# Recommendation tower with gathers, table looks and pairwise dot products: ten looked tables in eight straight-line groups of 256 samples, grams of one group placed between the looks of the next

## The reference, cut to what matters

```
e = stack([tbl_k[ids[:, k]] for k in range(26)], axis=1)        # 2048 x 26 x 128, fp32
combined = concat([dense[:, None, :], e], axis=1)               # 27 features of 128
inter = einsum('bnd,bmd->bnm', combined, combined)              # 27 x 27 a sample
z = concat([dense, inter[:, upper triangle]], axis=1)           # 351 pairs
h = concat([z, dense], axis=1)                                  # 607
h = relu(h @ W_top1 + b_top1)                                   # 512
h = relu(h @ W_top2 + b_top2)                                   # 256
y = h @ W_top3                                                  # 1
```

## Time and profile before

| what | value |
|---|---|
| median of 3 runs | 411.67 us (411.32 to 412.78) |
| the profiled execution | 414.85 us |
| its span, first to last instruction | 413.0 us |
| instructions in the profile | 14244 |
| mean granted TensorE clock | 0.971 |
| DMA traffic | 44.99 MB, mean 109 GB/s |
| packets under 512 B | 6198 of 20763 |

### The profile page before, as it was taken

One profiled execution on the slowest core, in us unless ns is written; L12 is line 12 of the kernel. 1 busy time (PEld: TensorE's weight loads), 2 busy tenths in 40 slices (PEclk: granted clock), 3 DMA queues, 4 the chain that ended last, 5 costly groups with the idle time before them and its releaser, 6 DMA issues.

```text
span 413.0 us, 14244 instructions
## 1 busy us (share of the span) xinstructions
PE 329.0 (80%) x6240; PEld 303.9 (74%) x6240; DVE 231.0 (56%) x234; ACT 142.9 (35%) x305; POOL 275.3 (67%) x295
## 2 busy tenths in 40 slices
PE   0300487999999999999989897989898895977676
PEld 0300486989898989897979796979888895966675
DVE  2244288686758676866666656576476656332211
ACT  1222216326333633363336231553236332442211
POOL 5777704777777777777777777777777777776000
PEclk9999998999999999999999998999999998998889
DMA  6444662254443434352424333342525142324020
GB/s 182 156 160 164 214 197 75 68 154 111 116 108 109 117 104 116 98 144 77 133 82 122 99 105 112 94 125 63 156 65 152 51 118 53 99 71 109 15 64 1
DMA packets 20763, 44.99 MB, mean 109 GB/s; under 512 B 6198, under 2 KB 11942, under 8 KB 20179
## 3 DMA queue, kind: packets, MB, share of 16 engines
q1 hardware_dynamic: 11524, 25.76, 20.3%
q0 software_dynamic: 9216, 18.89, 17.2%
HBM read 37.27 MB, written 7.36 MB: 108 GB/s over the span
## 4 chain that ended last, share of the span: by engine, by line
POOL 39%; PE 27%; issue 14%; DMA 7%; SPq 5%; ACT 4%; DVE 3%; POOLq 0%; ACTq 0%
POOL rows L294 39%; PE look_ps L333 11%; DMA grams<-in_table 6%; SPq L255 4%; PE gram_ps L354 4%; PE layer_ps L368 4%; PE layer_ps L379 3%; PE turn_ps L319 3%; ACT turned L576 2%; PE layer_ps L365 2%; DVE match L465 2%; DVE grams L451 1%; PE layer_ps L386 1%; DMA rows<-in_table,index 1%; ACT hidden L548 0%
## 5 line engine op out<-in xcount | busy, mean ns | idle before, releaser
L294 POOL DMA_INDIRECT rows<-in_table,index x288 | 274.5, 953 | 104.9 <-issue 86.5
L333 PE MATMUL look_ps<-match,table_high 125*128 125x256 f32 x512 | 137.9, 305 | 50.2 <-ACT looked_sb L564 27.7
L465 DVE TENSOR_TENSOR match<-look_ids,row_number_ps 125x2048 fp32r<-125x2048 int32 x64 | 145.8, 2280 | 6.5 <-DMA look_ids<-in_look_ids_rows 4.3
L333 PEld LDWEIGHTS look_ps<-match,table_high 125*128 125x128 f32 x512 | 103.2, 202 | 54.0 <-issue 52.4
L333 PE MATMUL look_ps<-match,table_low 125*128 125x256 f32 x512 | 132.2, 293 | 0.0
L333 PEld LDWEIGHTS look_ps<-match,table_low 125*128 125x128 f32 x512 | 103.8, 203 | 0.0
L451 DVE COPY grams<-gram_ps 27x432 f32<-27x432 f32 x64 | 38.2, 597 | 51.3 <-PE gram_ps L354 50.8
L319 PE MATMUL turn_ps<-identity,rows 128*128 128x128 f32 x288 | 47.2, 287 | 21.4 <-DMA rows<-in_table,index 21.3
L354 PE MATMUL gram_ps<-turned 128*27 128x27 f32 x4096 | 54.0, 194 | 5.1 <-issue 1.9
L354 PEld LDWEIGHTS gram_ps<-turned 128*27 128x27 f32 x4096 | 44.8, 105 | 15.4 <-issue 8.7
L368 PE MATMUL layer_ps<-pairs,w_pairs_sb 117*128 117x128 f32 x384 | 55.4, 282 | 0.0
(11 more groups left out here) (21 smaller groups left out, 101.8 us busy)
## 6 DMA issues: line engine op xcount, KB each, us to landing
look_ids<-in_look_ids_rows SPq DMA_DIRECT2D x16, 512.0 KB, 4.2
scratch<-grams SPq DMA_DIRECT2D x16, 364.5 KB
rows<-in_table,index POOLq DMA_INDIRECT x288
grams<-in_table SPq DMA_DIRECT2D x6, 500.0 KB
pairs<-scratch SPq DMA_DIRECT2D x48, 58.5 KB
scratch<-grams SPq DMA_DIRECT2D x16, 84.5 KB
dense_sb<-in_dense_t SPq DMA_DIRECT2D x1, 1024.0 KB, 5.0
turned<-in_table SPq DMA_DIRECT2D x2, 500.0 KB
```

The lines of the kernel that those rows point to most:

```text
L294: pool.indirect_dma_start(out=rows[u][:, group * GROUP_OF + n, :], out_offset=None, in_=tables[k], in_offset=bass.IndirectOffsetOnAxis(ap= ...
L333: last = nc.tensor.matmul(look_ps[:, 0:2 * P], part[0:look_rows, r, c, :], match[r % 2][0:look_rows, c, :], start=(c == 0 and part is tabl ...
L465: nc.vector.tensor_tensor(match[r % 2][0:look_rows], look_ids[0:look_rows, r].unsqueeze(1).broadcast_to(shape), row_number_ps[0:look_rows] ...
```

## The change

The order is new throughout, and so are the shapes:

- Ten tables are looked and 16 gathered. The features are reordered so that dense comes first, then the looked, then the gathered ones (`ORDER`), and the rows of `W_top1` with them.
- The unit of work is a group of 256 samples. There are eight, written out straight-line, with no loop in the program. `turned` exists twice, so looks are copied directly into it, two at a time from one of two PSUM banks.
- Transposed units and gram steps share three PSUM banks (`mid_ps`) in the order that `turn_number` and `gram_number` give. ScalarE makes all copies and activations; VectorE only matches and splits.
- A gram step still has 64 samples, now 16 from each quarter of the group, with 32 weight columns where 27 are features. So the four quadrants hold different samples, and `grams` is 128 partitions wide and exists once.
- The repack writes all 128 partitions (27 and 13 columns of 64 samples, 4 bytes each) and reads with 12 DMAs (3 chunks x 4 quadrants), each of 117 pieces of 64 samples. `scratch` and `pairs` exist once.
- Layers 1 to 3 run over 256 columns. The results are stored group by group.
- The raw tables are loaded in two parts, 112 and 13 partitions. The memory set aside for the descriptors of GpSimd's DMAs is 4096 bytes a partition.

```diff
-LOOKED = [8, 9, 10, 11, 15, 16, 17, 18]
+LOOKED = [8, 9, 10, 11, 15, 16, 17, 18, 19, 23]
+N = 256
+STEPS = 4
...
             def repack(g):
+                sp.wait_ge(mid_out, gram_number(g, STEPS - 1) + 1)
+                after(sp, pairs_in, PAIRS_DMAS * g)
+                flat = scratch.rearrange("s i j x -> (s i) j x")
+                sp.dma_start(flat[:, 0:FEATURES], grams[:]).then_inc(scratch_in, 16)
+                sp.dma_start(flat[:, FEATURES:WIDTH], grams[:, 0:SHIFTS]).then_inc(scratch_in, 16)
+                sp.wait_ge(scratch_in, SCRATCH_DMAS * (g + 1))
+                after(sp, layer1_done, 2 * g)
+                for c in range(CHUNKS):
+                    for s in range(QUADS):
+                        first = s * ROW * WIDTH + c * CHUNK_I * (WIDTH + 1) + 1
+                        skewed = bass.AP(scratch.tensor, first * IN_QUAD,
+                                         [[(WIDTH + 1) * IN_QUAD, CHUNK_I], [IN_QUAD, SHIFTS], [1, IN_QUAD]])
+                        sp.dma_start(pairs[0:CHUNK_ROWS, c, s * IN_QUAD:(s + 1) * IN_QUAD], skewed).then_inc(pairs_in, 16)
...
+            for j in range(groups * TILES):
+                for u in range(UNITS):
+                    after(pool, turn_done, UNITS * (j - 2) + u + 1)
...
+            def look(g, r):
+                pair = g * LOOK_PAIRS + r // 2
+                if g == 0:
+                    pe.wait_ge(tables_split, r + 1)
+                after(pe, looked, pair - 1)
+                pe.wait_ge(match_ready, g * LOOKS + r + 1)
...
+            def gram(g, k):
+                number = gram_number(g, k)
+                if k == 0:
+                    pe.wait_ge(mid_out, turn_number(g, TURNS - 1) + 1)
+                    pe.wait_ge(looked, LOOK_PAIRS * (g + 1))
+                    pe.wait_ge(dense_put, g + 1)
+                after(pe, mid_out, number - 2)
+                for i in range(IN_STEP):
+                    for s in range(QUADS):
+                        n = (s * IN_QUAD + k * IN_STEP + i) * FEATURES
+                        last = nc.tensor.matmul(
+                            mid_ps[number % 3][s * ROW:(s + 1) * ROW, i * FEATURES:(i + 1) * FEATURES],
+                            turned[g % 2][:, n:n + ROW], turned[g % 2][:, n:n + FEATURES], start=True, stop=True)
...
+            def layer1(g, o):
+                if o == 0:
+                    pe.wait_ge(pairs_in, PAIRS_DMAS * (g + 1))
...
+            for g in range(1, groups):
+                look(g, 0)
+                gram(g - 1, 0)
+                turn(g, 0)
+                look(g, 1)
+                gram(g - 1, 1)
+                turn(g, 1)
+                gram(g - 1, 2)
+                look(g, 2)
+                turn(g, 2)
+                gram(g - 1, 3)
+                look(g, 3)
+                turn(g, 3)
+                look(g, 4)
+                turn(g, 4)
+                look(g, 5)
+                turn(g, 5)
+                look(g, 6)
...
+                layer1(g - 1, 0)
+                layer1(g - 1, 1)
+                look(g, 7)
+                turn(g, 6)
+                layer1(g - 1, 2)
+                layer1(g - 1, 3)
+                look(g, 8)
+                turn(g, 7)
+                layer2(g - 1)
+                look(g, 9)
+                layer3(g - 1)
+            for k in range(STEPS):
+                gram(groups - 1, k)
+            for o in range(L1):
+                layer1(groups - 1, o)
+            layer2(groups - 1)
+            layer3(groups - 1)
```

More of the change, by code:

```diff
@@ L52, with build @@
 L2 = H2 // P
[L55 to L81, removed]
+def build(nc, dense_t, index_t, look_rows_t, tables, w1_dense, w1_pairs, b1, w2, b2, w3, y):
     fp32, fp32r, int32 = mybir.dt.float32, mybir.dt.float32r, mybir.dt.int32
@@ L85, in build @@
     batch = dense_t.shape[1]
[L86 to L92, removed]
+    groups = batch // N
+    table_rows = tables[LOOKED[0]].shape[0] // PARTS
+    assert batch % N == 0 and all(tables[k].shape[0] == table_rows * PARTS for k in LOOKED)
+    assert SPREAD < table_rows <= P and LOOKS % 2 == 0 and len(GATHERED) % UNIT_OF == 0 and FEATURES <= ROW
+    assert TURNS > STEPS and groups >= 2
     ctx = ExitStack()
@@ L388, in layer3 @@
                 last.then_inc(layer3_done, 1)
-            def tile(m, u, grams=True, layers=True, looks=True, last=False):
-                gm = m - 1 + u
-                for group in range(GROUPS):
-                    turn(m, u, group)
-                    if looks:
-                        for look_of in looks_after(m, u, group):
-                            look(*look_of)
-                    if grams and group < STEPS:
-                        gram(gm, 1 - u, group)
-                    if layers and group == AT_LAYER[0]:
-                        layer1(m - 1, u)
-                    if layers and group == AT_LAYER[1] and not last:
-                        layer2(m - 1, u)
-                    if layers and group == AT_LAYER[2] and not last:
-                        layer3(m - 1, u)
@@ L407, in _ @@
-            pe.wait_ge(identity_made, 1)
-            for r in range(EARLY):
-                look(0, r)
-            tile(0, 0, grams=False, layers=False)
-            tile(0, 1, layers=False)
-            pe.wait_ge(weights_summed, 1)
-            pe.wait_ge(dense_in, 16)
-            last_m = tiles // 2 - 1
-            with pe.Fori(1, last_m) as m:
-                tile(m, 0)
-                tile(m, 1)
-            tile(last_m, 0)
-            tile(last_m, 1, looks=False, last=True)
-            layer2(last_m - 1, 1)
@@ L623 @@
+            for k in range(STEPS):
+                take_gram(groups - 1, k)
+            for half in range(2):
+                relu1(groups - 1, half)
+            relu2(groups - 1)
+            copy_y(groups - 1)
 def kernel(**inputs):
```

600 lines of the change are left out of this document (266 added, 334 removed).

## The result

The changed kernel takes 488.08 us (median of 4 runs, 487.58 to 489.92) against 412.23 us for the kernel before in the same runs: a ratio of 1.185 (95% interval 1.180 to 1.189). It is slower, by 18% where 11% was forecast, and it lies 2 us outside the range given. Its profiled execution took 489.92 us for a span of 488.1 us.

What follows compares the result with a forecast made beforehand. TensorE was to bound the kernel, stalled each round by the pairs' way through DRAM: first pairs at 79.8 us, six rounds of 52.2, then the end, a span of 457.9; predicted 457 us, 11% slower, range 428 to 486.

Steps and rivals of the forecast that it cites:

- TensorE takes over from the gathers; VectorE and ScalarE are hidden.: Per round: TensorE needs 43.2 us, gathers 40.0; VectorE's 22.8 and ScalarE's 25 us fit behind TensorE.
- R = 17.1 us against 9.55 of cover.: Last gram to layer 1 through DRAM: copy 0.6, write 5.5, reads 8.6, last read 2.4; TensorE stalls 7.5 us a round.
- The doubling of the layer matmuls for 256 columns: Layers 1 to 3: 256 columns take twice the time of 128, at 0.87 ns a column.
- The scratch write at 257 GB/s.: Repack: writing 1.31 MB from 128 partitions over all 16 DMA engines takes 5.1 us plus 0.4 until bytes flow.
- the straight-line steps: Gram steps of a round: four cost 7.0 us, with no gaps, though the program has no loop any more.
- rival 4: Gram steps: straight-line instructions come late, a 1.91 us gap at each of four steps a round, 510 us; chance 0.04.
- its 33.6 us: TensorE's work in a round outside the cover of the pairs: 43.2 less 9.55 us.
- I add 1.5 us for each: Layer 1 behind each stall: TensorE runs at a lowered clock and loses 1.5 us.
- gram (0, 0) starts at 50.4 us: Prologue: group 0's gathers land at 45.8 us, then a turn 0.4 and two looks 4.2 us.
- The end.: After the last in-round pairs: rest of round 20.6, four gram steps 9.0, uncovered DRAM way 17.1, then 18.2 us.
- The range.: Whole kernel: 428 to 486 us leaves 2 in 10 out; the forecast's own part, 440 to 480, had chance 0.75.
- The low bound of R: Way of the pairs through DRAM with write 3.7 us and 0.40 us a read issue: given as 10.7 us.

Runs made afterwards that it cites:

- late: Changed kernel with layer 1 of a group moved behind look 9 and layers 2 and 3 into the next round: 430.35 us, 1.035.
- reads3: Changed kernel with only 3 of the 12 pair reads issued from group 1 on: 427.61 us, 1.025.
- spread: Kernel late with looks 2 and 3 moved ahead of gram steps 2 and 3: 430.8 us, 1.041.
- best: Changed kernel with layers 1 to 3 two rounds later, looks between gram steps, last gram steps interleaved with layer 1, late weights: 446.31 us, 1.079.
- burst: Kernel best with ids before pair reads and six last reads on ScalarE, but gram steps 1 and 2 close together again: 414.67 us, 0.999.
- peloop: Changed kernel with TensorE's groups 2 to 5 as a hardware loop of two groups: 488.15 us, 1.171.
- warm: Changed kernel with 56 extra matmuls ahead of the wait for the pairs, for all groups but the last: 474.86 us, 1.147.
- latew: Changed kernel with the 1.3 MB of weights loaded behind the ids of group 1: 487.05 us, 1.177.
- onedma: Changed kernel with each raw table loaded by one DMA of 125 partitions, as before: 510.23 us, 1.233.

## Why the prediction was wrong, step by step

The bottleneck, the main mechanism and the sign were right. The size was off by 30.2 us of span (488.1 against 457.9): 12.3 before the first pairs, 16.4 in six rounds, 1.5 at the end.

- **TensorE takes over from the gathers; VectorE and ScalarE are hidden.** Right: GpSimd waits 63.7 us for TensorE.
- **R = 17.1 us against 9.55 of cover.** Right: 17.2 us in the round shown, 17.1 in the next (237.81 to 254.91), 17.5 in the mean. Its terms were right to within 0.5 us in the round shown, where two errors cancel: 5.1 for the write (5.5 forecast), 9.05 for the eleven reads (8.6), 2.4 for the last. Over the eight groups the write takes 4.5 to 6.3 us and the last landing 2.2 to 3.3. late and reads3 each took this wait away by a different end and got 58 and 60 us back. The doubling of the layer matmuls for 256 columns held: 0.43 for two and 1.30 for six at full clock.
- **The scratch write at 257 GB/s.** Right, and it goes with the rule that the prediction takes from the Trainium skill (DMA: Bandwidth & Descriptors, "Why a DMA increments its semaphore by 16 and not by 1"), by which a transfer of 128 partitions is spread over all 16 engines. The trace agrees: with 128 partitions the DMA share is 0.96 at 369 GB/s from 185 to 189 us, gathers included, where 27 partitions had 0.56 at 144 GB/s.
- **"the straight-line steps" and rival 4.** This is the step that failed in the rounds: the forecast put a round at 52.2 us with no gaps between gram steps in it, and gave rival 4, instructions that come late, a chance of 0.04. The gaps are real: 14.7 us in the seven rounds, 2.1 a round, and not 7.6. The cause that rival 4 names is borne out by the timing: every gap of the changed kernel ends 1.25 to 1.60 us after a load of instructions, and they grow and shrink with the density of short matmuls (spread, best, burst). No run took the loads away from this kernel, so the last proof is missing. peloop, meant as that test, kept them. What was wrong in the price is the frequency: a step with a look ahead of it mostly pays nothing or under 1 us, one close behind another step pays 1.3 to 2.1. The earlier trace rows showed it: two steps took 4.5 us where two separate ones take 3.5. I had used that row for the end of the kernel, and not for steps 1 and 2 of a round, which are nearly as close. The reason given against the rival, that the prologue is straight-line too, did not carry: in that prologue a look stands between any two gram steps.
- **"I add 1.5 us for each".** Mis-sized: the clock costs 1.9 us a stall (warm), 2.3 in the round shown (5.75 against 3.46 us for half of layer 1). A round is 2.7 us longer than forecast. The gaps give 2.1 of it, the clock 0.4 to 0.8 and R 0.4; that is a little more than 2.7, so the rest of a round ran slightly under its 33.6 us.
- **"gram (0, 0) starts at 50.4 us".** Mis-sized: it starts at 57.95, and the first pairs arrive at 92.1 and not at 79.8, 12.3 us late. The row for a gather's landing was taken at the end of the old kernel, where the DMA engines are idle; in the new prologue their share is near 1.0 for most of the first 44 us. But latew freed them at 40 us and moved the start by 1.4 us only, so what holds the start is open. Another 4.4 us are lost between the first gram and the last: gaps, and a look at the half clock, 3.62 us in place of 1.92, behind the gap at 66.28 us.
- **The end.** 66.4 us from the last layer 1 in a round to the end, 64.9 forecast. That it is so close is in part luck: the four gram steps end to end took 12.0 us and not 9.0, with three gaps in them, while R was 16.0 and not 17.1.
- **The range.** It ended at 486. The forecast's own part of it, 440 to 480, was made from R alone, the term that was right; the terms that the trace did not bound, the prologue and the gaps, had no room in it. (The low bound of R is also added up wrongly: 0.6 + 3.7 + 4.4 + 2.4 is 11.1 and not 10.7. Nothing measured came near it.)

## What to carry to other kernels

When data go through DRAM and back inside one loop round, write the way out term by term (copy, write, issues of the reads times their number, last landing) and lay it against the work that stands between in the program; here the order of a few lines was worth 58 us. Count too what queues behind those issues on the same engine: the ids behind the reads cost 44 us in a version whose pairs were fully hidden. Ten looked tables and groups of 256 do pay (0.967 of the time before), once layer 1 is a round later, the ids go ahead of the reads and a long instruction stands between bursts of short ones; the versions tried show this for the whole, not for each part. When a loop is written out, look at the queue that loads instructions: a test by a loop is one only if that queue falls silent in it.

## What the runs showed of the hardware

- A DMA read of 117 pieces takes 0.74 us of the issuing queue, 0.78 with the time to the next, with pieces of 512 bytes (before) and of 256 bytes (after) alike.
- TensorE's instructions come in DMA packets of 16 KB, 48 of them in the straight-line kernel. Two gram steps (256 short matmuls) nearly in a row mostly bring a pause of 0.4 to 2.2 us, which ends 1.25 to 1.64 us after such a packet has landed (after and peloop). With a look of 2 us between two steps the pause was mostly under 1 us or absent, but 1.23 us once in the changed kernel and 1.98 us once in reads3.
- A hardware loop of one round (the kernel before) loads no instructions from 120 to 346 us; one of two rounds (peloop) keeps loading, 50 packets in all.
- 392 matmuls whose result is thrown away made a kernel 13.2 us faster: behind the stalls the clock is 0.50 without them, and layer 1 up to its third quarter takes 1.9 us more in the mean.
- Two DMAs of 112 and 13 partitions bring the first three 512 KB tables 2.2 and 2.9 us apart; with one DMA of 125 partitions they come 5 us apart (onedma).
